# The two attention phases: the engines' programs written out straight instead of running in loops

## Chip, core and metric

The kernel runs on one core of one Trainium2 chip. Time is the device time of one launch, in microseconds (us); what stands for a version is the median of its runs. An engine's instructions run in the order in which its program gives them, and engines meet at semaphores.

## What is computed

The input is eight sequences of 512 tokens with 128 features. Two layers follow each other. Each adds to x an attention with 16 heads of 8 features, and a second branch. Layer 0 has an amplitude and phase attention, and beside it an attention over the batch followed by a mixture of eight experts; layer 1 has plain causal attention and a mixture of the best two of eight experts.

```
x = L0_attn_x
xn = _layernorm(x, axis=-1)
x = x + _L0_attn_ref(xn, ...) + _L0_ffn_ref(xn, ...)
xn = _layernorm(x, axis=-1)
x = x + _L1_attn_ref(xn, ...) + _L1_ffn_ref(xn, ...)
...
scores = jnp.where(mask[None, None], scores, -jnp.inf)     # causal, 512 x 512
attn = jax.nn.softmax(scores, axis=-1)
out = jnp.einsum('bhqk,bhkd->bhqd', attn, v)
```

## The kernel before

Seven phases run one after the other (`setup, mix0, middle0, attend0, middle1, experts1, attend1`), each a block that all engines enter and leave together. The change touches `attend0` and `attend1`, which are one function, `attend`, called with layer 0 or 1.

A **unit** is a group of four heads of one sequence. There are 32 (`UNITS`), four to a sequence, and a sequence is called a **row**. Every engine's program is cut into **steps**; step t does work for several units at once, at different depths of a pipeline:

- PE computes the scores of unit t that give each query's largest score (`maxima`, L2131 and the mask L2143), the scores of unit t-2 the other way round (`probabilities`, L2163), the product with the values for t-3 (`mix`, L2176), and turns the result of t-4 (`turn_mix`, L2184). At the end of a row it turns (L2190) and projects (`project`, L2196) the row's result.
- ACT takes ten exponentials of 128x512 in a step (L2089, unit t-2), and then copies the mixed result of t-3 (`mixT`, L2114). This copy stands once in each step, at its end, so its starts mark the steps. At the end of a row ACT also copies `contextT` (L2102). In layer 0 it makes, one row late, four normalised tiles (`z_norm`, L2107).
- DVE reduces the maxima (L2255, L2258, L2260, L2261), splits those of unit t-1 (`split_maxima`, L2271 and L2273) at the start of the step, copies them (L2280), divides (`divide`, L2287 and L2291), and ends a row with `add_row` (L2304; in layer 1 L2308), which adds the projection to x. In layer 0 it takes the statistics of the second norm as well.
- GpSimd (POOL) masks the exponentials (L2052), copies the values (L2060), and issues one indirect DMA in a step of layer 0 (L2068), two in layer 1. In layer 0, once in a row, it follows this with an addition over 128x512 (`second_norm`, L2022).
- SyncE (SP) loads the stacked q and k of unit t (L1973) and moves the maxima of t-3 into place (L1963).

GpSimd's program has always been written out, step by step. The other four use `in_steps`: the first steps straight, then a loop on the engine whose body is 8 steps (two rows), then the rest straight. For PE, ACT and DVE steps 0 to 7 are straight, 8 to 31 are three passes of the loop, and what follows is straight. SP does so too in layer 1; in layer 0 its steps 0 to 15 are straight and 16 to 31 are two passes. Step numbers of this text are those of t. In a loop the pass's number is in a register, so that a wait for a count that grows with the unit needs its target computed first, and so does an address that depends on the row:

```
    with eng.Fori(0, turns) as i:
        for phase in range(cycle):
            step(Unit(i + first // cycle, phase, cycle))
...
        dve.wait_ge(x_in[u.row_par].sem, (r - u.row_par) * 8 + 16)
        dve.tensor_tensor(k.x_sum[:, here, :], proj, x_tile[:, u.row_par, :, :], ALU.add).then_inc(added.sem, 1)
```

Of the kernel before, what the change touches and what calls it, by code (L numbers as in the profile page):

```python
# [43 lines left out]
NG = NH // GH  # L44
# [103 lines left out]
def in_steps(eng, units, depth, step, cycle=2, first=4):  # L148

    turns = (units - first) // cycle
    for t in range(first):
        step(Unit(t // cycle, t % cycle, cycle))
    with eng.Fori(0, turns) as i:
        for phase in range(cycle):
            step(Unit(i + first // cycle, phase, cycle))
    for t in range(first + cycle * turns, units + depth - 1):
        step(Unit(t // cycle, t % cycle, cycle))


def active(t, k, units):

    return not isinstance(t.turn, int) or 0 <= t.n - k < units
# [1698 lines left out]
def attend(nc, k, layer):  # L1863
# [5 lines left out]
    UNITS = B * NG  # L1869
# [7 lines left out]
    with ExitStack() as ctx:  # L1877
# [40 lines left out]
        DEPTH = 6  # L1918
        Z_AFTER = 12
# [35 lines left out]
        def _(sp):  # L1955
# [35 lines left out]
                    sp.dma_start(k.out[bass.ds(u.row, 1), :, :].rearrange("b (j p) d -> p (b j) d", p=P),  # L1991
                                 k.x_sum[:, bass.ds(u.row * QT, QT), :]).then_inc(stored[u.row_par].sem, 16)

            if layer == 0:
                in_steps(sp, UNITS, Z_AFTER + 1, step, 2 * NG, 4 * NG)
            else:
                in_steps(sp, UNITS, DEPTH + 1, step, 2 * NG, 2 * NG)
            if layer == 1:
                for i in range(2):
                    sp.wait_ge(stored[i].sem, B // 2 * 16)  # L2000
# [82 lines left out]
        @block.scalar  # L2083
        def _(act):
            def exponentials(u, c, side):
                act.wait_ge(prob_ps.sem, prob_ps.after(u, 2 * c + side))
                if c == 0 and side == 0 and u.past(2):
                    act.wait_ge(mixed.sem, mixed.done(u - 2))
                act.activation(probs[:, u.par, 2 * c + side, :], ps[:, PROB + side, :], ACT.Exp, scale=SCALE ** -2)\  # L2089
                   .then_inc(exped.sem, 1)  # L2090

            def step(t):
                row_ends = active(t, 4, UNITS) and (t - 4).group == NG - 1
                for c in range(SCH):
                    if active(t, 2, UNITS):
                        for side in range(2):
                            exponentials(t - 2, c, side)
                    if c == 3 and row_ends:
                        r = (t - 4).row
                        act.wait_ge(context_turned.sem, context_turned.done(r))  # L2100

                        act.copy(contextT[:, :], ps[:, TURN, :]).then_inc(contextT_ready.sem, 1)  # L2102
                    if c == 1 and layer == 0 and active(t, 6, UNITS) and (t - 6).group == NG - 1:
                        r = (t - 6).row
                        act.wait_ge(z_shift_done.sem, z_shift_done.done(r))
                        for j in range(QT):
                            act.activation(z_norm[:, j, :], z_sum[:, j, :], ACT.Identity, bias=z_shift[:, j:j + 1],  # L2107
                                           scale=z_rstd[:, j:j + 1]).then_inc(z_normed.sem, 1)
                if active(t, 3, UNITS):
                    u = t - 3  # L2110
                    act.wait_ge(mixed.sem, mixed.done(u))
                    if u.past(1):
                        act.wait_ge(mix_turned.sem, mix_turned.done(u - 1))
                    act.copy(mixT[:, :], ps[:, MIX, :]).then_inc(mixT_ready.sem, 1)  # L2114

            in_steps(act, UNITS, DEPTH + 1 - layer, step, 2 * NG, 2 * NG)

        @block.tensor
        def _(pe):
# [119 lines left out]
                    if c == 4 and row_ends:  # L2239
                        project(t - 4)  # L2240

            in_steps(pe, UNITS, DEPTH, step, 2 * NG, 2 * NG)

        @block.vector
        def _(dve):
# [64 lines left out]
            def step(t):  # L2310
                z_row = layer == 0 and active(t, 5, UNITS) and (t - 5).group == NG - 1
                if active(t, 1, UNITS):
                    split_maxima(t - 1)
                for c in range(MCH):
                    if active(t, 0, UNITS):
                        reduce(t, c)
                    if c == 0 and active(t, 4, UNITS):
                        divide(t - 4)
                    if c == 1 and active(t, 1, UNITS):
                        copy_maxima(t - 1)  # L2320
                    if c == 2 and z_row:
                        ln_stats(dve, z_sum, z_stats, z_mv, z_stats_done, z_mv_done, (t - 5).row, z_summed)
                    if c == 4 and z_row:
                        r = (t - 5).row
                        dve.wait_ge(z_rstd_done.sem, z_rstd_done.done(r))
                        dve.scalar_tensor_tensor(out=z_shift[:, :], in0=z_mv[:, :, 0], scalar=-1.0, in1=z_rstd[:, :],
                                                 op0=ALU.mult, op1=ALU.mult).then_inc(z_shift_done.sem, 1)
                if active(t, 4, UNITS) and (t - 4).group == NG - 1:
                    add_row(t - 4)

            in_steps(dve, UNITS, DEPTH, step, 2 * NG, 2 * NG)


def attend0(nc, k):
# [81 lines left out]
```

## Time and profile before

| | us |
|---|---|
| median of 3 runs (1272.55 to 1272.88) | 1272.88 |
| the profiled execution's own time | 1268.47 |
| its span, first to last instruction | 1266.9 |
| PE busy (77% of the span) | 981.7 |
| DVE busy (65%) | 819.4 |
| ACT busy (55%) | 690.9 |
| POOL busy (46%) | 582.5 |

The span is what the trace covers; 1.6 us of the profiled execution lie outside it. An engine counts as busy in its instructions proper, and not in those that compute registers, wait or branch, so these show only as time in which the engine stands still. The two attentions run from about 388 to 673 us and from about 1000 to the end. The granted TensorE clock averages 0.897 of full speed over the span.

### The profile page before, as it was taken

The numbers are of one execution on the slowest core, as the hardware profiler recorded it, in microseconds if no ns is written. First come the engines' busy times: TensorE is split into PE (matmuls) and PEld (weight loads), VectorE is DVE, ScalarE is ACT, GpSimd is POOL, SyncE is SP. The second block draws the span as 40 slices with busy tenths as digits, with TensorE's granted clock in tenths as the row PEclk, the third lists the DMA queues.
The fourth block names the chain that finished last, engine by engine and source line by source line (L and its number), as shares of the span: only waits on it lengthen the run. The fifth ranks groups of instructions, "written<-read, shape, count | busy, mean of one in ns | idle before, by whom it ended". The sixth has DMA issues, their size and how long they took to land. (4 is left out here: it accounts for less than half of the span.)

```text
span 1266.9 us, 27743 instructions
## 1 busy us (share of the span) xinstructions
PE 981.7 (77%) x8908; PEld 647.1 (51%) x8908; DVE 819.4 (65%) x1770; ACT 690.9 (55%) x1325; POOL 582.5 (46%) x793
## 2 busy tenths in 40 slices
PE   3789652989867988888872655199999599999987
PEld 1456431777753544444431433188888345555553
DVE  1566341667748999999943776133333699999992
ACT  1366343878714777677763454022222277777775
POOL 3467537010112565565551466411110367777775
PEclk9899776999985999999996666599999599999999
DMA  4321042577752222222201434456665112211111
GB/s 134 108 51 51 26 118 74 160 210 225 208 172 77 80 69 69 72 76 62 73 24 36 115 115 119 142 164 194 185 192 163 39 46 54 55 52 51 51 45 30
DMA packets 151735, 126.30 MB, mean 100 GB/s; under 512 B 23760, under 2 KB 134272, under 8 KB 151648
## 3 DMA queue, kind: packets, MB, share of 16 engines
q1 hardware_dynamic: 141904, 107.05, 29.5%
q0 software_dynamic: 8016, 17.71, 4.8%
q8 instruction: 44, 0.72, 0.2%
q10 hardware_dynamic: 1728, 0.46, 0.2%
q14 instruction: 43, 0.35, 0.1%
HBM read 77.83 MB, written 44.70 MB: 97 GB/s over the span
## 5 line engine op out<-in xcount | busy, mean ns | idle before, releaser
L2089 ACT ACTIVATE attend_probs<-attend_attend_ps 128x512 f32<-128x512 f32 x640 | 351.1, 600 | 161.7 <-PE attend_attend_ps L2163 154.4
L2163 PE MATMUL attend_attend_ps<-attend_q,attend_ks 50*128 50x512 f16 (+3 forms) x1024 | 236.5, 307 | 20.1 <-ACT attend_probs L2089 18.0
L2052 POOL TENSOR_SCALAR_AFFINE_SELECT attend_probs<-attend_probs 128x512 f32<-128x512 f32 x256 | 158.7, 637 | 159.5 <-ACT attend_probs L2089 158.6
L2131 PE MATMUL attend_attend_ps<-attend_ks,attend_q 48*128 48x512 f16 (+3 forms) x1024 | 191.3, 317 | 25.5 <-DMA attend_ks<-k_stack 16.2
L2176 PE MATMUL attend_attend_ps<-attend_probs,attend_vals 128*32 128x512 f32 (+3 forms) x2048 | 178.9, 446 | 0.0
L2258 DVE TENSOR_REDUCE attend_neg_max<-attend_attend_ps 128x2 f32<-128x1024 f32 x128 | 155.0, 1211 | 9.9 <-PE attend_attend_ps L2143 9.8
L2143 PE MATMUL attend_attend_ps<-identb,stairs 64*128 64x128 bf16 (+1 forms) x1280 | 144.3, 213 | 0.0
L2163 PEld LDWEIGHTS attend_attend_ps<-attend_q,attend_ks 50*128 50x128 f16 x1024 | 70.9, 94 | 116.1 <-ACT attend_probs L2089 93.2
L2260 DVE TENSOR_REDUCE attend_neg_max<-attend_attend_ps 128x2 f32<-128x768 f32 x128 | 121.8, 951 | 9.2 <-PE attend_attend_ps L2143 8.4
L1800 DVE TENSOR_TENSOR experts_hidden<-experts_experts_ps,experts_gate 128x512 f32<-128x512 f32 x39 | 27.0, 691 | 136.3 <-ACT experts_gate L1779 136.3
L2143 PEld LDWEIGHTS attend_attend_ps<-identb,stairs 64*128 64x128 bf16 x1280 | 105.9, 100 | 17.5 <-issue 4.7
L1834 PE MATMUL experts_experts_ps<-experts_rowsT,experts_w_in 128*128 128x256 f32 (+1 forms) x468 | 110.1, 385 | 1.6 <-ACT experts_rowsT L1787 1.5
L1104 POOL DMA_INDIRECT sorted<-middle_scaled,rank_row x64 | 66.6, 1040 | 58.1 <-issue 28.9
L1834 PEld LDWEIGHTS experts_experts_ps<-experts_rowsT,experts_w_in 128*128 128x128 f32 (+1 forms) x468 | 82.4, 183 | 17.6 <-ACT experts_rowsT L1787 2.1
L1779 ACT ACTIVATE experts_gate<-experts_experts_ps 128x512 f32<-128x512 f32 x39 | 23.3, 597 | 120.8 <-PE experts_experts_ps L1834 120.8
L1766 POOL DMA_DIRECT2D experts_rows<-sorted x39 | 27.7, 712 | 131.8 <-issue 131.8
L2131 PEld LDWEIGHTS attend_attend_ps<-attend_ks,attend_q 48*128 48x128 f16 x1024 | 67.2, 96 | 39.0 <-DMA attend_ks<-k_stack 16.6
L2255 DVE TENSOR_REDUCE attend_neg_max<-attend_attend_ps 128x4 f32<-128x1024 f32 x64 | 78.3, 1224 | 8.5 <-PE attend_attend_ps L2143 8.5
L1430 POOL TENSOR_TENSOR x_sum<-middle_amp_n,middle_sine 128x1024 f32<-128x1024 f32 x8 | 18.9, 2365 | 118.4 <-DVE middle_amp_n L1636 118.3
L2068 POOL DMA_INDIRECT attend_moe<-done,back_row x64 | 61.6, 962 | 14.9 <-issue 14.9
L1846 PE MATMUL experts_experts_ps<-experts_w_out,experts_hidden 128*128 128x128 f32 (+1 forms) x468 | 58.7, 275 | 0.9 <-DVE experts_result L1811 0.9
L2176 PEld LDWEIGHTS attend_attend_ps<-attend_probs,attend_vals 128*32 128x32 f32 x2048 | 44.7, 109 | 22.8 <-issue 5.9
(319 smaller groups left out, 1950.7 us busy)
## 6 DMA issues: line engine op xcount, KB each, us to landing
experts_w_in<-in_L_ffn_w_dram SPq DMA_DIRECT2D x78, 176.0 KB, 2.4
q_stack<-middle_parts SPq DMA_DIRECT2D x24, 256.0 KB, 3.3
k_stack<-middle_parts SPq DMA_DIRECT2D x24, 256.0 KB, 3.6
attend_q<-q_stack SPq DMA_DIRECT2D x64, 96.0 KB, 2.2
attend_ks<-k_stack SPq DMA_DIRECT2D x64, 96.0 KB, 2.2
middle_w_in<-in_L_ffn_W_dram SPq DMA_DIRECT2D x23, 256.0 KB, 2.7
middle_w_out<-in_L_ffn_W_dram SPq DMA_DIRECT2D x23, 256.0 KB, 3.1
experts_rows<-sorted POOLq DMA_DIRECT2D x39, 128.0 KB, 2.5
```

The source lines that it names most:

```text
L1104: pool.indirect_dma_start(k.sorted1, bass.IndirectOffsetOnAxis(ap=k.rank_row[:, c * NT + tile:c * NT + tile + 1], axis=0), scaled[:, c, ti ...
L1834: mm = pe.matmul(ps[0:size[c], hidden_bank(u, bank), half * ROWS:(half + 1) * ROWS], w_in[:, u.phase, w + c * P:w + c * P + size[c]], rows ...
L2052: pool.affine_select(out=block_, in_=block_, compare_op=ALU.is_ge, fill=0.0, base=0, pattern=[[0, GH], [1, P]], channel_multiplier=-1).the ...
L2068: pool.indirect_dma_start(moe[:, c * NT + n, :], None, src, bass.IndirectOffsetOnAxis(ap=at_row[:, c * NT + n:c * NT + n + 1], axis=0))\
L2089: act.activation(probs[:, u.par, 2 * c + side, :], ps[:, PROB + side, :], ACT.Exp, scale=SCALE ** -2)\
L2131: pe.matmul(ps[:, bank + side, col:col + (qt + 1) * P], q[rows(side, KR), g, pair, qt * P:(qt + 1) * P], ks[rows(side, KR), g, pair, 0:(qt ...
L2143: mm = pe.matmul(span[:, :, col:col + 64], k.stairs[here, stair:stair + P], k.identb[here, here].unsqueeze(1).broadcast_to([64, len(blocks ...
L2163: mm = pe.matmul(ps[:, PROB + side, col:col + S - kt * P], ks[rows(side, KM), g, pair, kt * P:(kt + 1) * P], q[rows(side, KM), g, pair, kt ...
L2176: mm = pe.matmul(ps[32 * h:32 * h + 32, MIX, kt * P:S], vals[:, u.par, kt * GH + h, :], probs[:, u.par, 2 * c + h % 2, col:col + S - kt * ...
L2255: ins = dve.tensor_reduce(out[:, :, :, 1], pair_banks.rearrange("p s (h t) -> p s h t", h=HP), X_AXIS, ALU.max, negate=True)
L2258: ins = dve.tensor_reduce(out[:, :, c // 2, 3], pair_banks, X_AXIS, ALU.max, negate=True)
L2260: dve.tensor_reduce(out[:, :, c // 2, 2], pair_banks[:, :, 0:384], X_AXIS, ALU.max, negate=True)
```

## The change

The loop is dropped from the four programs that used it: each step is given constant numbers. The loops of other phases stay.

```diff
@@ -156,6 +156,11 @@
     for t in range(first + cycle * turns, units + depth - 1):
         step(Unit(t // cycle, t % cycle, cycle))
 
 
+def all_steps(units, depth, step, cycle):
+    for t in range(units + depth - 1):
+        step(Unit(t // cycle, t % cycle, cycle))
+
+
...
-            if layer == 0:
-                in_steps(sp, UNITS, Z_AFTER + 1, step, 2 * NG, 4 * NG)
-            else:
-                in_steps(sp, UNITS, DEPTH + 1, step, 2 * NG, 2 * NG)
+            all_steps(UNITS, Z_AFTER + 1 if layer == 0 else DEPTH + 1, step, 2 * NG)
...
-            in_steps(act, UNITS, DEPTH + 1 - layer, step, 2 * NG, 2 * NG)
+            all_steps(UNITS, DEPTH + 1 - layer, step, 2 * NG)
...
-            in_steps(pe, UNITS, DEPTH, step, 2 * NG, 2 * NG)
+            all_steps(UNITS, DEPTH, step, 2 * NG)
...
-            in_steps(dve, UNITS, DEPTH, step, 2 * NG, 2 * NG)
+            all_steps(UNITS, DEPTH, step, 2 * NG)
```

No instruction that computes changes its place. What goes are the register instructions (REGISTER_ALU, and ISA, which is several of them in one) and the branches. In the lists that follow, a semaphore has the name under which its number was first used. On DVE, the end of the loop's last step, which ends a row, and the start of the next step before the change (here `setup_raw_in7` is `projected`, `setup_raw_in5` is `x_in`, and `setup_scale_ready` is `max_turned`):

```order
L2255 TENSOR_REDUCE attend0_neg_max<-attend0_attend_ps 128x4 [waits attend0_scored]
L2299 ISA
L2303 ISA [waits setup_raw_in7]
L2304 ISA [waits setup_raw_in5]
L2304 TENSOR_TENSOR x_sum<-attend0_attend_ps,attend0_x_tile 128x512
L155 REGISTER_ALU
L155 COMPARE_AND_BRANCH
```

At the loop's top stand two more before the first instruction of `split_maxima`:

```order
L155 ISA
L2270 ISA [waits setup_scale_ready]
L2271 TENSOR_SCALAR attend0_max_parts<-attend0_neg_max 128x2x8 [waits setup_roots_ready]
```

The same place on DVE in the changed kernel, where lines after 1990 stand 2 further down:

```order
L2257 TENSOR_REDUCE attend0_neg_max<-attend0_attend_ps 128x4 [waits attend0_scored]
L2306 TENSOR_TENSOR x_sum<-attend0_attend_ps,attend0_x_tile 128x512 [waits setup_raw_in5,setup_raw_in7]
L2273 TENSOR_SCALAR attend0_max_parts<-attend0_neg_max 128x2x8 [waits setup_roots_ready,setup_scale_ready]
L2275 SCALAR_TENSOR_TENSOR attend0_max_parts<-attend0_neg_max,attend0_max_parts 128x2x8 [waits setup_norms_ready]
```

The three register instructions between the reduction and the addition are gone, and the waits stand on the addition itself. On PE, the loop's top with the start of its first step before the change (`setup_turned` is `max_in`, `setup_raw_in6` is `added`, `setup_copied` is `context_done`):

```order
L155 ISA
L2160 ISA [waits setup_turned]
L2163 MATMUL attend0_attend_ps<-attend0_q,attend0_ks 128x512 [waits setup_cols_in]
L2124 ISA
L2126 ISA [waits attend0_loaded0]
L2131 MATMUL attend0_attend_ps<-attend0_ks,attend0_q 128x512 [waits setup_roots_ready]
L2131 MATMUL attend0_attend_ps<-attend0_ks,attend0_q 128x512
L2143 MATMUL attend0_attend_ps<-identb,stairs 128x64 x4
L2163 MATMUL attend0_attend_ps<-attend0_q,attend0_ks 128x512 [waits setup_cols_in]
L2204 REGISTER_ALU
L2208 ISA [waits setup_copied]
L2182 REGISTER_ALU [waits setup_raw_in6]
```

The same stretch of PE in the changed kernel, with the instruction that comes next:

```order
L2165 MATMUL attend0_attend_ps<-attend0_q,attend0_ks 128x512 [waits setup_cols_in,setup_turned]
L2133 MATMUL attend0_attend_ps<-attend0_ks,attend0_q 128x512 [waits setup_roots_ready,attend0_loaded0]
L2133 MATMUL attend0_attend_ps<-attend0_ks,attend0_q 128x512
L2145 MATMUL attend0_attend_ps<-identb,stairs 128x64 x4
L2165 MATMUL attend0_attend_ps<-attend0_q,attend0_ks 128x512 [waits setup_cols_in]
L2186 MATMUL attend0_attend_ps<-ident,attend0_mixT 128x128 [waits setup_raw_in13,setup_raw_in6,setup_copied]
```

Seven register instructions are gone, and every wait stands on the matmul it is for.

## Rows read from the trace of the kernel before

**Rows 1.** Waits by engine (us in total, times, longest us): ACT's largest.

```profile
ACT attend_probs L2089 <- PE attend_attend_ps L2163: 154.4, 203, 24.6
```

**Rows 2.** Waits of SP's queue, the largest.

```profile
SPq L1963 <- DVE attend_maxT L2280: 197.7, 64, 7.7
```

**Rows 3.** Timeline of ACT, layer 0: start us, us, instruction. Steps 5 to 24.

```profile
425.12 0.59 ACT L2114 COPY attend_mixT<-attend_attend_ps 128x512 f32<-128x512 f32 x1
432.36 0.59 ACT L2114 COPY attend_mixT<-attend_attend_ps 128x512 f32<-128x512 f32 x1
...
440.17 0.61 ACT L2114 COPY attend_mixT<-attend_attend_ps 128x512 f32<-128x512 f32 x1
...
448.04 0.59 ACT L2114 COPY attend_mixT<-attend_attend_ps 128x512 f32<-128x512 f32 x1
...
456.46 0.59 ACT L2114 COPY attend_mixT<-attend_attend_ps 128x512 f32<-128x512 f32 x1
...
472.56 0.61 ACT L2114 COPY attend_mixT<-attend_attend_ps 128x512 f32<-128x512 f32 x1
...
480.51 0.59 ACT L2114 COPY attend_mixT<-attend_attend_ps 128x512 f32<-128x512 f32 x1
...
489.56 0.59 ACT L2114 COPY attend_mixT<-attend_attend_ps 128x512 f32<-128x512 f32 x1
...
505.57 0.61 ACT L2114 COPY attend_mixT<-attend_attend_ps 128x512 f32<-128x512 f32 x1
...
515.64 0.59 ACT L2114 COPY attend_mixT<-attend_attend_ps 128x512 f32<-128x512 f32 x1
...
573.74 0.61 ACT L2114 COPY attend_mixT<-attend_attend_ps 128x512 f32<-128x512 f32 x1
...
583.50 0.59 ACT L2114 COPY attend_mixT<-attend_attend_ps 128x512 f32<-128x512 f32 x1
```

**Rows 4.** Timeline of ACT, layer 1, steps 11 to 13.

```profile
1083.97 0.61 ACT L2114 COPY attend_mixT<-attend_attend_ps 128x512 f32<-128x512 f32 x1
...
1091.96 0.59 ACT L2114 COPY attend_mixT<-attend_attend_ps 128x512 f32<-128x512 f32 x1
...
1099.21 0.59 ACT L2114 COPY attend_mixT<-attend_attend_ps 128x512 f32<-128x512 f32 x1
```

**Rows 5.** Timelines of ACT and DVE, ends of rows at steps 7 and 11.

```profile
438.72 0.59 ACT L2102 COPY attend_contextT<-attend_attend_ps 128x512 f32<-128x512 f32 x1
...
440.71 0.68 DVE L2304 TENSOR_TENSOR x_sum<-attend_attend_ps,attend_x_tile 128x512 f32<-128x512 f32 x1
...
471.10 0.59 ACT L2102 COPY attend_contextT<-attend_attend_ps 128x512 f32<-128x512 f32 x1
...
473.23 0.69 DVE L2304 TENSOR_TENSOR x_sum<-attend_attend_ps,attend_x_tile 128x512 f32 x1
```

**Rows 6.** Timelines of DVE and POOL, starts of steps 12, 16, 24 and 32.

```profile
473.79 0.97 POOL L2068 DMA_INDIRECT attend_moe<-done,rank_row  x1 [0.16 <-issue]
474.04 0.17 DVE L2273 SCALAR_TENSOR_TENSOR attend_max_parts<-attend_neg_max,attend_max_parts 128x16 f16<-128x16 f32 x1
...
506.81 0.97 POOL L2068 DMA_INDIRECT attend_moe<-done,rank_row  x1 [0.16 <-issue]
507.27 1.86 DVE L2271 TENSOR_SCALAR attend_max_parts<-attend_neg_max 128x16 f16<-128x16 f32 x1
...
575.35 1.93 DVE L2273 SCALAR_TENSOR_TENSOR attend_max_parts<-attend_neg_max,attend_max_parts 128x16 f16<-128x16 f32 x1
...
643.23 1.96 DVE L2273 SCALAR_TENSOR_TENSOR attend_max_parts<-attend_neg_max,attend_max_parts 128x16 f16<-128x16 f32 x1
```

**Rows 7.** PE's loop branch (count, ns least, median, most), all loops of the program.

```profile
L155 PEldq COMPARE_BRANCH  x13: 76/208/234, 504.9 to 1239.6; - x13
```

**Rows 8.** DMA queues, 410 to 510 us, then 511 to 641: packets, MB, share.

```profile
q8 instruction: 9, 0.15, 0.6%
...
q14 instruction: 2, 0.02, 0.0%
```

## The prediction, made before the changed kernel ran

> **What bounds the kernel now.** I read the waits first. ACT's largest wait is for PE's second scores, 154.4 us in 203 pieces [rows 1]: in the attentions PE and ACT run as a ring, in which an exponential waits for its scores and the next scores wait for the exponential to free their bank. DVE stands in that ring once in a step, since PE waits for its quotients, split maxima and, at a row's end, its addition. SP's queue waits 197.7 us for DVE, at most 7.7 us at a time [rows 2]; it is early everywhere.
>
> Then I measured the ring, from one `mixT` copy of ACT to the next, which is one step. A plain step takes 432.36 - 425.12 = 7.24 us in the straight part of layer 0 [rows 3], and 1099.21 - 1091.96 = 7.25 us inside the loop of layer 1 [rows 4]. PE, ACT and DVE compute registers before nearly every wait in the second and never in the first. So in a plain step all of them lie under other work: an engine's queue computes them while its last instruction runs. What a loop costs has to be looked for where an engine comes late to a wait that is already met, which is at the ends of rows.
>
> **The end of a row.** PE projects, DVE adds (L2304), and PE waits for that addition in the next step before `turn_mix`. From the start of ACT's `contextT` copy to the start of the addition it takes 440.71 - 438.72 = 1.99 us at step 7, which is straight, and 473.23 - 471.10 = 2.13 us at step 11, in the loop [rows 5]: 0.14 us for the register instructions that stand between the projection and the addition. The step that follows takes 448.04 - 440.17 = 7.87 us at step 8 and 480.51 - 472.56 = 7.95 us at step 12 [rows 3], in layer 1 at step 12 1091.96 - 1083.97 = 7.99 us [rows 4]. Step 8 still pays the way into the loop, so it is an upper bound of the straight step; 7.95 - 0.14 = 7.81 less what the loop adds on PE's side is the other bound. I take 7.80, a saving of 0.15 to 0.19 us, say 0.18, at each of steps 12, 16, 20, 24, 28 and 32 of both layers: **12 x 0.18 = 2.2 us**.
>
> **The turn of the loop.** PE's branch takes 208 ns in the median and 76 at the least, which is one not taken [rows 7]; PE turns twice in each attention, and a row's end is where it happens. I allow 0.08 us for each of the 4 turns and 0.08 for each of the 2 ways in: **0.5 us**. But in layer 0 the turning steps take far more: step 16 is 515.64 - 505.57 = 10.07 us and step 24 is 583.50 - 573.74 = 9.76, against 7.95 for step 12, which is the same step in the middle of the body [rows 3]. This is not the branch. At step 12 POOL starts its indirect DMA at 473.79, and the second instruction of DVE's split starts 0.25 us later and takes 0.17 us. At step 16 DVE's first one comes 0.46 us after the DMA's start and takes 1.86 us for the same 16 columns; at step 24 the DMA, by the same 1.23 us behind `mixT` as at step 12, starts at 574.97, and DVE's second one comes 0.38 us behind and takes 1.93; at step 32 the same instruction takes 1.96 [rows 3, 6]. POOL goes from the DMA straight into its 128x512 addition, and the DVE instruction ends when that ends. So there is a cliff somewhere between 0.25 and 0.38 us behind the DMA's start: DVE ahead of it runs at once, and DVE behind it waits for both of POOL's instructions, with PE and ACT waiting behind DVE. POOL's program has no loop and keeps its distance from ACT. DVE's register instructions push it over.
>
> Without them DVE is 0.14 us earlier than at step 12, which puts its second instruction at 0.25 - 0.14 = 0.11 us, well ahead of the cliff, in all rows. Steps 16 and 24 then cost what step 12 does: 10.07 - 7.95 = 2.12 and 9.76 - 7.95 = 1.81 us. At step 32 the pipeline drains and PE has no maxima to compute, so part of the stall is slack; between nothing and 1.8 us I take half, 0.9. **Together 4.8 us**, no part of which is counted above, where these steps give only their 0.18.
>
> The Trainium skill (SBUF — State Buffer, Who interferes with whom) says that DVE and GpSimd share a pair of SBUF ports under an exclusive lock that whoever starts first holds for its whole instruction. The two waits of nearly 2 us agree with a lock. That the lock is held from the DMA's start does not agree with step 12, where DVE ran in 0.17 us inside it; by that rule DVE would be stopped at 0.11 us as well, nothing of the 4.8 us would come back, and the sum would be 2.7. The measured step decides.
>
> **SP, ACT and the rest.** SP loses its address computations beside each DMA; its 197.7 us of waiting cover them [rows 2]. ACT's register instructions lie under exponentials of 0.6 us, by the plain steps above: nothing. If that cover were gone, plain steps would differ between loop and straight, and they do not. The fill of the pipeline (steps 0 to 7) and its drain are straight already.
>
> **What is added is code to fetch.** An instruction queue, q8, moved 9 packets from 410 to 510 us, while code ran for the first time, and none from 511 to 641, in the second and third pass, where only q14 appears with 2 [rows 8]. So the body was there already, and the straight program must bring in about 9 more packets per 100 us of it: some 13 in each attention, 26 in all. Their share of 0.6% of 16 engines over 100 us is 1.07 us for each packet. They come about 11 us apart, and the plain step of 7.24 us lies in the stretch with fetches. So I cost them at nothing; what hides them is that a packet is wanted only 10 us after the last.
>
> **Sum.** 2.2 + 0.5 + 4.8 = 7.5 us, less 0.3 for small new stalls where engines meet earlier than before: 7.2. From the profiled execution's 1268.47 this gives 1261.3. The median of the runs is 4.4 us above that execution, which the trace does not explain; taken off the median, **1265.7 us**.
>
> **A race that can go either way.** Step 9 takes 456.46 - 448.04 = 8.42 us, step 13 489.56 - 480.51 = 9.05 [rows 3]. They hold the same work, and DVE and POOL want to go at the same moment there; five of the six such steps are long. The change moves neither against the other, since both hang on DVE's statistics. All six may come out short (3.2 us less) or all long (0.6 more).
>
> **Rivals.**
> - *The collision stays.* Another delay, or the cliff lying lower, keeps DVE behind POOL in the same three steps: 2.2 + 0.5 = 2.7 us, 1270.2. For it speaks that only an interval of 0.13 us is known to hold the cliff; against it, that steps 8 and 12 both pass. Chance 0.09.
> - *More collisions go than the trace shows.* Steps 12, 20 and 28 stand at most 0.13 us ahead of the cliff, and the unprofiled runs are 4.4 us longer, which is about two more collisions of 2.1. Then 4.2 more come back: 1261.5. Chance 0.12.
> - *Slower: the fetch stalls PE.* Should each of the 26 new packets keep PE waiting for its 1.07 us, that is 28 us against 7.2 of gain: 1293. It decides from 7.2 / 26 = 0.28 us per packet. Against it speaks the plain step with fetches. Chance 0.06.
> - *The loop's turn costs a fetch.* The Trainium skill (Runtime: NRT & Kernel Launch, Instruction fetch mechanics) says that a taken branch to code outside a small window waits for a DMA fetch. For four turns of PE at 1.07 us this kernel would lose 4.3 us that the change returns, beside the 7.2: 1261.4. No q8 packet in the passes and a branch of at most 234 ns speak against it [rows 7, 8]. Chance 0.02.
> - *Nothing to be seen:* the stalls move elsewhere in the ring, and the time stays within 2.5 us. Chance 0.06.
>
> That leaves 0.65 for the forecast, with a range of its own of 1262 to 1268. Over all, 1259 to 1271 holds eight in ten: below it lie more collisions together with a won race, above it the fetch. A measurement of this kernel tells about 0.2%, 2.5 us, from no change. Faster by more is the forecast, the two cases that give more, and half of the first rival: 0.84. Within it 0.10, slower 0.06.
>
> **What would show it.** In the profile after, steps 16 and 24 of layer 0 last 7.8 us, and L2273 and L2275 (the split's new lines) stay under 0.3 us at the starts of rows; the addition begins 1.99 us behind `contextT` at every row's end; plain steps stay at 7.24; q8 has about 70 packets instead of 44. I am wrong if plain steps grow, if a 1.9 us instruction of the split turns up at a row's start, or if PE stands idle around q8's packets for a reason that no semaphore gives.

## The result, and the profile after

The changed kernel takes 1263.9 us in the median of 6 runs (1263.0 to 1266.6), the kernel before beside it on the same chip (A) 1272.6 (6 runs, 1270.6 to 1272.9). The ratio is 0.9939 [0.9927, 0.9952], which is 7.8 us less.

The profiled execution took 1266.19 us with a span of 1264.6, only 2.3 us less than the one profiled before. The page of the changed kernel, the lines that moved:

```profile
span 1264.6 us, 25739 instructions
...
PE 987.7 (78%) x8908; PEld 649.9 (51%) x8908; DVE 810.1 (64%) x1770; ACT 691.2 (55%) x1325; POOL 580.4 (46%) x793
...
q8 instruction: 67, 1.10, 0.4%
```

The profile before counts 27743 instructions, so some 2000 register instructions and branches are gone, and the instructions proper have kept their numbers. DVE is 9.3 us less busy with the same 1770 instructions. Of that, 7.0 us are in the two instructions of the split (30.7 + 15.9 us before, 25.9 + 13.7 after), which are as many as before and were held less. q8 moved 23 packets more.

Timeline of ACT in the changed kernel (start us, us, instruction), layer 0: `contextT` and `mixT` of step 7, `mixT` of steps 8, 9, 11, 12, 13, then `contextT` and `mixT` of step 15, `mixT` of 16, 23 and 24:

```profile
440.24 0.59 ACT L2104 COPY attend_contextT<-attend_attend_ps 128x512 f32<-128x512 f32 x1
...
441.69 0.61 ACT L2116 COPY attend_mixT<-attend_attend_ps 128x512 f32<-128x512 f32 x1
...
449.50 0.59 ACT L2116 COPY attend_mixT<-attend_attend_ps 128x512 f32<-128x512 f32 x1
...
457.89 0.59 ACT L2116 COPY attend_mixT<-attend_attend_ps 128x512 f32<-128x512 f32 x1
...
473.87 0.61 ACT L2116 COPY attend_mixT<-attend_attend_ps 128x512 f32<-128x512 f32 x1
...
481.68 0.59 ACT L2116 COPY attend_mixT<-attend_attend_ps 128x512 f32<-128x512 f32 x1
...
490.67 0.59 ACT L2116 COPY attend_mixT<-attend_attend_ps 128x512 f32<-128x512 f32 x1
...
505.20 0.59 ACT L2104 COPY attend_contextT<-attend_attend_ps 128x512 f32<-128x512 f32 x1
...
506.65 0.61 ACT L2116 COPY attend_mixT<-attend_attend_ps 128x512 f32<-128x512 f32 x1
...
514.46 0.59 ACT L2116 COPY attend_mixT<-attend_attend_ps 128x512 f32<-128x512 f32 x1
...
572.18 0.61 ACT L2116 COPY attend_mixT<-attend_attend_ps 128x512 f32<-128x512 f32 x1
...
580.00 0.59 ACT L2116 COPY attend_mixT<-attend_attend_ps 128x512 f32<-128x512 f32 x1
```

From one `mixT` start to the next: step 8 takes 449.50 - 441.69 = 7.81 us, step 12 also 7.81, step 16 514.46 - 506.65 = 7.81 where it took 10.07, step 24 7.82 where it took 9.76 [rows 3]. All ends of rows now look like step 8. Step 13 takes 490.67 - 481.68 = 8.99 against 9.05 [rows 3].

Timelines of DVE and POOL in the changed kernel, start of step 16, in order of time:

```profile
507.19 0.68 DVE L2306 TENSOR_TENSOR x_sum<-attend_attend_ps,attend_x_tile 128x512 f32<-128x512 f32 x1
507.79 0.17 DVE L2273 TENSOR_SCALAR attend_max_parts<-attend_neg_max 128x16 f16<-128x16 f32 x1
507.88 0.97 POOL L2070 DMA_INDIRECT attend_moe<-done,rank_row  x1 [0.16 <-issue]
507.99 0.17 DVE L2275 SCALAR_TENSOR_TENSOR attend_max_parts<-attend_neg_max,attend_max_parts 128x16 f16<-128x16 f32 x1
508.88 1.29 POOL L2024 TENSOR_TENSOR attend_z_sum<-y_all,attend_moe 128x512 f32<-128x512 f32 x1
```

The addition starts 507.19 - 505.20 = 1.99 us behind `contextT`, and the second instruction of the split 0.11 us behind the DMA's start. The two instructions of the split last 0.17 us each, where L2271 lasted 1.86 [rows 6]. The second comes 0.10 to 0.11 us behind the DMA's start in all seven rows.

Where the time went, from the same `mixT` starts and the ends of the spans, in us. "After" is the execution above, the last two columns are profiled executions of both kernels on two slower chips that the experiments used:

| stretch | before | after | before, chip B | after, chip D |
|---|---|---|---|---|
| start to step 3 of layer 0 | 410.7 | 412.2 | 411.9 | 412.1 |
| layer 0, steps 8 to 32 | 209.8 | 203.4 | 209.9 | 204.0 |
| layer 0, steps 33 and 34 | 11.6 | 13.3 | 11.6 | 14.2 |
| to step 3 of layer 1 | 360.8 | 361.9 | 364.1 | 362.9 |
| layer 1, steps 8 to 32 | 195.0 | 193.5 | 210.2 | 204.1 |
| layer 1, steps 33 and 34 | 10.7 | 12.0 | 13.5 | 12.1 |

On the first chip the steps give 6.4 + 1.4 = 7.8 us. In this execution 2.9 of them are given back in the drains, where the pipeline empties, and 2.6 in stretches whose code did not change; the first stretch alone differs by up to 9 us between executions with the same code in it (406.1 to 415.2 over the runs below), which is why a difference of two single executions says little here.

The drain of layer 0, the stretch from the second last `mixT` copy to the last, as granted clock (`PEclk`, 1.00 is 2.4 GHz) and busy time of each engine. Before:

```profile
core 0: us, PE busy (x) PEld busy (x) DVE busy (x) ACT busy (x) POOL busy (x), PEclk, DMA share, GB/s
657.80:661.60 3.80, 2.92 (x36) 1.31 (x36) 0.55 (x2) 0.67 (x3) 3.51 (x4) 1.00 0.00 0
```

After:

```profile
652.91:658.33 5.42, 4.61 (x36) 1.84 (x36) 0.55 (x2) 0.60 (x3) 4.37 (x4) 0.69 0.07 17
```

The same 36 matmuls take 4.61 us of PE instead of 2.92, and the granted clock averages 0.69 over the stretch, which is 1.2 GHz for more than half of it, instead of 2.4 GHz throughout (1.00). In the second drain it is 0.79 from 1244.2 to 1252.5.

### The profile page after: what moved, and what is told of

It reads as the page before. It is cut to its first block and busy times, and to the rows that moved or that the text cites. A ratio compares the mean times of both kernels' runs of the same rounds, so it can differ in the third digit from the quotient of the medians.

```text
span 1264.6 us, 25739 instructions
## 1 busy us (share of the span) xinstructions
PE 987.7 (78%) x8908; PEld 649.9 (51%) x8908; DVE 810.1 (64%) x1770; ACT 691.2 (55%) x1325; POOL 580.4 (46%) x793
## 5 line engine op out<-in xcount | busy, mean ns | idle before, releaser
L2260 DVE TENSOR_REDUCE attend_neg_max<-attend_attend_ps 128x2 f32<-128x1024 f32 x128 | 155.0, 1211 | 10.2 <-PE attend_attend_ps L2145 10.1
```

The lines of the kernel that those rows point to most:

```text
L2260: ins = dve.tensor_reduce(out[:, :, c // 2, 3], pair_banks, X_AXIS, ALU.max, negate=True)
```

## The experiments

Eleven runs followed on three chips more: eight edited kernels, the kernel before once and the changed kernel twice. Each ratio is against the kernel before on the same chip, which took 1291.4 us on that of the first four (chip B), 1270.2 on that of the next four (C) and 1292.5 on that of the last three (D).

**e1, DVE alone straight.** On the kernel before, one of the four programs changed:

```diff
-            in_steps(dve, UNITS, DEPTH, step, 2 * NG, 2 * NG)
+            all_steps(UNITS, DEPTH, step, 2 * NG)
```

> The kernel before with DVE's two attention programs alone written out straight; PE, ACT and SP keep their loops. My theory (DVE's register instructions at a row's end make it miss the gap before GpSimd's addition): the addition starts 1.99 us behind contextT at every row's end, steps 16 and 24 of layer 0 fall from 10.07 and 9.76 us to about 7.9, no instruction of the split over 1 us at a row's start, and most of the gain is here: 5.5 to 7 us, 1265.5 to 1267 against a before of 1272.6. Rival (the loop's turn itself, above all PE's branch, costs the time): steps 16 and 24 stay near 10 us and the time within 2 us of before.

Measured: 1285.3, ratio 0.9941 [0.9919, 0.9963]. ACT's timeline, `mixT` of steps 15 and 16 of layer 0, then of 14 and 15 of layer 1:

```profile
506.25 0.61 ACT L2119 COPY attend_mixT<-attend_attend_ps 128x512 f32<-128x512 f32 x1
...
514.12 0.59 ACT L2119 COPY attend_mixT<-attend_attend_ps 128x512 f32<-128x512 f32 x1
...
1112.07 0.59 ACT L2119 COPY attend_mixT<-attend_attend_ps 128x512 f32<-128x512 f32 x1
...
1122.36 0.62 ACT L2119 COPY attend_mixT<-attend_attend_ps 128x512 f32<-128x512 f32 x1
```

Step 16 takes 7.87 us with PE, ACT and SP still looping. DVE's loop alone was what put it into the collisions. The 0.06 us above 7.81 is what remains of the turn on the other engines. Layer 1's step 15, which ends a row, takes 10.29 us here. On the first chip it took 8.78 before the change:

```profile
1106.44 0.59 ACT L2114 COPY attend_mixT<-attend_attend_ps 128x512 f32<-128x512 f32 x1
...
1115.22 0.61 ACT L2114 COPY attend_mixT<-attend_attend_ps 128x512 f32<-128x512 f32 x1
```

So layer 1 runs in another regime on this chip, of which the runs below show more.

**e2, all straight but DVE.** On the changed kernel, DVE's call turned back.

```diff
-            all_steps(UNITS, DEPTH, step, 2 * NG)
+            in_steps(dve, UNITS, DEPTH, step, 2 * NG, 2 * NG)
```

> The changed kernel with DVE's programs alone put back into the loop; PE, ACT and SP are straight. My theory: DVE is late again, x is added 2.13 us behind contextT in the loop and 2.25 at its turn, steps 16, 24 and 32 of layer 0 collide and steps 16 and 24 last 9.7 us or more; the time is within 2 us of before, 1270.5 to 1272.5. Rival (what PE, ACT and SP no longer compute gives the gain): steps 16 and 24 near 7.9 us, about 1266.

Measured: 1287.3, ratio 0.9956 [0.9932, 0.9981]. ACT's timeline at the same four places, with DVE's split instruction at the start of step 16:

```profile
505.03 0.61 ACT L2116 COPY attend_mixT<-attend_attend_ps 128x512 f32<-128x512 f32 x1
...
506.73 1.85 DVE L2273 TENSOR_SCALAR attend_max_parts<-attend_neg_max 128x16 f16<-128x16 f32 x1
...
514.93 0.59 ACT L2116 COPY attend_mixT<-attend_attend_ps 128x512 f32<-128x512 f32 x1
...
1113.58 0.59 ACT L2116 COPY attend_mixT<-attend_attend_ps 128x512 f32<-128x512 f32 x1
...
1123.08 0.62 ACT L2116 COPY attend_mixT<-attend_attend_ps 128x512 f32<-128x512 f32 x1
```

In layer 0 it is the kernel before: step 16 takes 9.90 us, with 1.85 in the split, step 24 takes 9.64, and steps 8 to 32 take 209.3 together. With e1 this settles the 4.8 us of layer 0. The time did not stay near that of before, as I had expected, for a reason in layer 1: its step 15 takes 9.50 us instead of the 10.29 of e1, and of the other five steps of the loop that end a row four take the same; one, step 19, takes 10.18.

**e3, a sweep over the cliff.** In the changed kernel DVE writes a single column of a spare tile r times behind the addition of row r, to come later by a little more each row.

```diff
+                    for n in range(r):
+                        dve.memset(pad[:, 4 * n:4 * n + 1], 0.0)
```

> The changed kernel with r tiny writes of one column (memset) put on DVE behind the addition that ends row r of layer 0, r from 0 to 7, so that DVE starts the split later and later from row to row; everything else as it was. If each takes about 60 ns, the split's second instruction comes 0.10, 0.16, 0.22, 0.28, 0.34, 0.40 and 0.46 us behind the start of GpSimd's indirect DMA. Theory (a cliff between 0.25 and 0.38 us): steps 8, 12, 16 stay at 7.8 to 7.9 us, and from some row on between the fourth and the fifth a split instruction takes 1.9 us and the step 9.7 or more, all later rows too. Rival (the time lost grows with DVE's lateness, no cliff): each row-end step is 0.06 us longer than the one before and none jumps.

Measured in one profiled execution: 1286.3. Each write took only some 10 ns, so the second split instruction came 0.10 to 0.16 us behind the DMA's start, none was held, and all those steps stayed at 7.81 to 7.82. It says nothing of the cliff; e6 repeats it with five times the writes.

**before_again.** The kernel before, unchanged.

> The kernel before, unchanged, for a second profile: the unprofiled median of before lies 4.1 us above its profiled execution. If the collisions of layer 0 differ from execution to execution, more row-end steps than 16, 24 and 32 last 9.7 us or more here. If the clock makes the difference, the steps are the same and the granted clock or the phases outside the attentions differ. If neither differs, profiling itself makes the executions shorter. Time: 1270.5 to 1273, ratio 1.00.

Measured: 1292.6, ratio 0.9995 [0.997, 1.002]. ACT's timeline, layer 1, `mixT` of steps 13 to 15:

```profile
1109.35 0.59 ACT L2114 COPY attend_mixT<-attend_attend_ps 128x512 f32<-128x512 f32 x1
...
1117.15 0.59 ACT L2114 COPY attend_mixT<-attend_attend_ps 128x512 f32<-128x512 f32 x1
...
1127.41 0.62 ACT L2114 COPY attend_mixT<-attend_attend_ps 128x512 f32<-128x512 f32 x1
```

In layer 0 the same three steps collide as in the first profile, by the same amounts (10.04, 9.78, 8.35 us), and no others. So the collisions are a fixed pattern. Layer 1 is slower here: step 14, a plain one, takes 7.80 us, and step 15, which ends a row, 10.26, where the first chip had 7.23 and 8.78. The steps behind the ends of rows are no longer than on the first chip (7.95 to 8.01 us against 7.98 to 8.06). Step 7 ends a row too, but in the part that is straight in this kernel as well, and takes 9.51. The granted clock is 1.00 in this stretch on both chips, so it is not that.

**after_again.** The changed kernel, unchanged.

> The changed kernel once more, beside runs of before on the same chip. On the chip of the first four experiments layer 1 ran differently from the first profiles: a plain step took 7.75 us and not 7.23, and the step that ends a row 10.27 us with PE and ACT in loops against 9.50 without. If this is a property of the chip, then on such a chip the change gains the two parts together, near 1.0%, and on one like the first 0.6%. If it comes from profiling or from one kernel's code, layer 1 is as in the first profile after, wherever this runs. The drain steps (33 and 34) were 3 us longer in the first profile after, with the clock at 1.2 GHz there; if that is the change's doing it shows again here.

Measured: 1262.8, ratio 0.9947 [0.9928, 0.9965]. Every step from 8 to 32 of both layers is within 0.02 us of the first profile of the changed kernel, and the last step of layer 0 takes 5.32 us again instead of 3.72: the lower clock in the drains comes back with it.

**e4, the second norm's work moved later.** The race of steps 9, 13, 17 and so on was to be taken apart: in the changed kernel POOL computes the reciprocal deviation behind its masks, ACT makes `z_norm` at its fourth place in the step, not its second, and DVE computes the shift one step later.

```diff
                 pool.tensor_tensor(z_sum[:, :, :], k.y[:, here, :], moe[:, here, :], ALU.add).then_inc(z_summed.sem, 1)
-                ln_rstd(pool, k, z_mv, z_ve, z_rstd, z_mv_done, z_eps_done, z_rstd_done, r)
...
+                if layer == 0 and n >= 6 and (n - 6) % NG == 0:
+                    ln_rstd(pool, k, z_mv, z_ve, z_rstd, z_mv_done, z_eps_done, z_rstd_done, (n - 6) // NG)
...
-                    if c == 1 and layer == 0 and active(t, 6, UNITS) and (t - 6).group == NG - 1:
+                    if c == 3 and layer == 0 and active(t, 6, UNITS) and (t - 6).group == NG - 1:
```

> The changed kernel with the second norm of layer 0 moved off the start of the step after a row's end: GpSimd computes z_rstd after the masks of its unit instead of before them, DVE makes z_shift in the next step behind its second reduction and no longer ahead of the split, ACT normalises two chunks later. Theory (in steps 13, 17, 21, 25 and 29 the split waits for GpSimd's masks, which stand one behind the other there because z_rstd held them up): these steps fall from 8.98 us to 8.4 or less and the split's first instruction takes under 0.3 us; 3 us less than the changed kernel, 0.25%. Rival (the long step is ACT's four extra tiles and no wait for DVE): no change, or slower because the norm is used later.

Measured: 1265.7, ratio 0.9976 [0.9959, 0.9992], 2.9 us above the changed kernel on the same chip. DVE's timeline, start of step 13:

```profile
479.53 0.17 DVE L2274 TENSOR_SCALAR attend_max_parts<-attend_neg_max 128x16 f16<-128x16 f32 x1
479.74 0.17 DVE L2276 SCALAR_TENSOR_TENSOR attend_max_parts<-attend_neg_max,attend_max_parts 128x16 f16<-128x16 f32 x1
```

In the changed kernel these two take 0.68 and 0.55 us here; now no instruction of the split is held anywhere in layer 0. Yet step 13 still takes 9.0 us. Step 9 became as long, steps 10, 14, 22 and 26 grew from 8.16 to 8.8, and 18 and 30 fell to 7.2. The theory had these steps at 8.4 us or less once the split runs free, and they are not; the edit moved work of ACT too, so it does not price the hold by itself. The rival, ACT's four extra tiles (1.64 us of ACT in such a step), is left and fits, but no run leaves them out.

**e5, the addition away from the DMA.** On the kernel before, with all its loops, POOL's `second_norm` goes behind the step's first mask.

```diff
-                if layer == 0 and n >= 6 and (n - 6) % NG == 0:
-                    second_norm((n - 6) // NG)
-                if n < UNITS:
-                    for i in range(QT):
+                for i in range(QT):
+                    if n < UNITS:
                         mask(n, i)
+                    if i == 0 and layer == 0 and n >= 6 and (n - 6) % NG == 0:
+                        second_norm((n - 6) // NG)
```

> The kernel before, all loops kept, with one thing changed on GpSimd: in layer 0 its 128x512 addition and what follows of the norm stand behind the first mask of the step and no longer directly behind the indirect DMA. Theory (DVE, late, waits for the DMA and for the addition that follows without a gap): the split still comes late at steps 16, 24 and 32 but waits for the rest of the DMA at most, 0.6 us instead of 1.9, or not at all if only the addition holds it up; steps 16 and 24 last 8.0 to 8.6 us instead of 10.0 and 9.8, 3 to 5 us less in all, 0.3%. Rival (the loop's turn costs it by itself): they stay near 10 us.

Measured: 1265.2, ratio 0.9967 [0.995, 0.9983]. Timelines of DVE, POOL and ACT around the start of step 16, with `mixT` of steps 15 and 16 first and last:

```profile
507.01 0.61 ACT L2114 COPY attend_mixT<-attend_attend_ps 128x512 f32<-128x512 f32 x1
...
508.24 0.97 POOL L2068 DMA_INDIRECT attend_moe<-done,rank_row  x1 [0.16 <-issue]
...
508.70 0.17 DVE L2271 TENSOR_SCALAR attend_max_parts<-attend_neg_max 128x16 f16<-128x16 f32 x1
508.91 0.18 DVE L2273 SCALAR_TENSOR_TENSOR attend_max_parts<-attend_neg_max,attend_max_parts 128x16 f16<-128x16 f32 x1
...
511.63 1.28 POOL L2022 TENSOR_TENSOR attend_z_sum<-y_all,attend_moe 128x512 f32<-128x512 f32 x1
...
515.40 0.59 ACT L2114 COPY attend_mixT<-attend_attend_ps 128x512 f32<-128x512 f32 x1
```

DVE comes 0.46 us behind the DMA's start, exactly as late as in the collision of before [rows 6], and runs in 0.17 us; the second comes 0.67 behind and runs in 0.18. The DMA does not hold DVE at all. What held it was the addition queued behind the DMA; whether another GpSimd instruction in that place would hold it too was not tried. Step 16 takes 8.39 us instead of 10.07, which is 0.43 more than step 12; DVE still comes late there. Steps 8 to 32 of layer 0 take 203.9, nearly what the change itself reaches, while the loops still run; part of that is in steps 13, 17 and so on. Step 13 fell from 9.05 to 8.70.

**e6, the sweep again.** As e3 with `range(5 * r)`.

> As e3_sweep, where one tiny write delayed DVE by only some 10 ns, so that no row reached the cliff; here 5r of them behind the end of row r: the split's second instruction about 0.10, 0.15, 0.20, 0.25, 0.30, 0.35 and 0.40 us behind the DMA's start. Theory: none of the first four is held, the last one is, and every row behind the first held one too; the held step lasts 9.7 us or more against 7.8. Rival (no cliff): the steps grow by 0.05 us each.

Measured in one profiled execution: 1271.3. Timelines of POOL and DVE at the start of step 16 and of step 20:

```profile
506.68 0.97 POOL L2071 DMA_INDIRECT attend_moe<-done,rank_row  x1 [0.16 <-issue]
...
506.93 0.18 DVE L2276 SCALAR_TENSOR_TENSOR attend_max_parts<-attend_neg_max,attend_max_parts 128x16 f16<-128x16 f32 x1
...
539.61 0.97 POOL L2071 DMA_INDIRECT attend_moe<-done,rank_row  x1 [0.16 <-issue]
...
539.94 1.99 DVE L2276 SCALAR_TENSOR_TENSOR attend_max_parts<-attend_neg_max,attend_max_parts 128x16 f16<-128x16 f32 x1
...
540.60 1.29 POOL L2025 TENSOR_TENSOR attend_z_sum<-y_all,attend_moe 128x512 f32<-128x512 f32 x1
```

At 0.25 us behind the DMA's start it runs in 0.18 us and the step takes 7.82; at 0.33 us it is held 1.99 us, until the addition has ended (539.94 + 1.99 = 541.93 against 540.60 + 1.29 = 541.89), and the step takes 9.64. The next two rows come at 0.42 and 0.46 us and take 9.64 each, and in the last the first split instruction already comes at 0.33 us and is held. Less than 0.1 us of delay costs 1.8 us. But this sweep has only the step from 10 writes to 15 there, and e8 below finds that 15 writes delay DVE by themselves. Free of such writes, the trace of the kernel before has the bounds 0.26 us (not held, step 28) and 0.37 (held, step 32).

The Trainium skill (SBUF — State Buffer, Who interferes with whom) has an exclusive lock between DVE and GpSimd, which whoever issues first holds for the whole instruction. The trace agrees that one waits until the other's instruction has ended. Taken by the starts in the trace, the rule does not hold: at 539.94 DVE was there 0.66 us before the addition started, with nothing but the DMA running on POOL. Whether the addition counted as issued by then, behind the DMA, no run shows.

**e7, both.** The changed kernel with the edit of e5.

> The changed kernel with the move of e5 on top: GpSimd's 128x512 addition of layer 0 stands behind the first mask. Theory: steps 16, 24 and 32 have no collision to lose any more, so only the steps after a row's end gain: in e5 step 13 took 8.70 us against 9.05 before, so steps 13, 17, 21, 25 and 29 fall from 8.98 to about 8.7, 1.5 us in all; about 0.7% under the kernel before, 1261 where that takes 1270. Rival: the race of these steps falls the other way and nothing is gained, the same as the changed kernel.

Measured: 1274.1, ratio 0.9857 [0.9834, 0.988], the best of all. ACT's timeline, steps 12 and 13 of layer 0:

```profile
476.66 0.59 ACT L2116 COPY attend_mixT<-attend_attend_ps 128x512 f32<-128x512 f32 x1
...
485.30 0.59 ACT L2116 COPY attend_mixT<-attend_attend_ps 128x512 f32<-128x512 f32 x1
```

Step 13 takes 8.64 us where the changed kernel has 8.98, and steps 8 to 32 of layer 0 take 201.7, 2.3 less than in the changed kernel on this chip. That is all that the profile puts down to the edit. The medians are 7.0 us apart; the rest isn't traced to it (this execution's stretch ahead of layer 0's step 3 was 407.1 against 412.1, and that code is the same). Two of the steps that end a row in layer 1, 15 and 23, took 10.2 us here and not 9.5.

**after_third.** The changed kernel on the same chip as e7.

> The changed kernel, unchanged, beside e7 on the same chip: ratio 0.994 to the kernel before; in the profile the steps of the first one, 7.81 us behind each row's end.

Measured: 1281.1, ratio 0.9915 [0.9887, 0.9943], 11.0 us less than before by the ratio, more than on the first chip. The table above has where: against the kernel before on chip B, which is as slow, 5.9 us come from layer 0 and 6.1 from layer 1 instead of 1.4. Layer 1's steps 11, 15 and so on take 9.51 us instead of 10.27. In layer 0 the steps behind the ends of rows are those of the first profile, as expected, but step 9 is long this time, 8.97 us.

**e8, the sweep with the addition moved.** The edits of e6 and e5 together, on the changed kernel.

> The delays of e6 with the move of e5: GpSimd issues its indirect DMA in the same place, but a mask follows and not the addition. If the addition holds DVE up before it has started, none of the seven rows is held, at any delay, and the steps behind the ends of rows grow smoothly from 7.8 to about 8.1 us. If the DMA itself has a part in it (its writing of descriptors), the rows from 0.34 us on are still held, for 0.6 us at most.

Measured in one profiled execution: 1277.2. Timelines of POOL and DVE at the start of step 24:

```profile
567.23 0.97 POOL L2071 DMA_INDIRECT attend_moe<-done,rank_row  x1 [0.16 <-issue]
567.44 0.17 DVE L2274 TENSOR_SCALAR attend_max_parts<-attend_neg_max 128x16 f16<-128x16 f32 x1
...
568.57 0.17 DVE L2276 SCALAR_TENSOR_TENSOR attend_max_parts<-attend_neg_max,attend_max_parts 128x16 f16<-128x16 f32 x1 [0.95 <-DVE attend_max_parts L2274]
...
570.06 1.27 POOL L2025 TENSOR_TENSOR attend_z_sum<-y_all,attend_moe 128x512 f32<-128x512 f32 x1
```

No instruction of the split was held for 1.9 us, in any row, which agrees with e5. But from the fourth row on, whose writes are 15 and more, DVE is late without a holder: here the second instruction starts 0.95 us behind the end of the first, and starts while POOL stands idle between the DMA's end at 568.20 and its next mask at 569.46. Steps 20 to 32 take 8.07, 8.83, 8.99 and 7.52. I put that down to the burst of tiny writes, which no run shows by itself, so the later rows of this sweep tell nothing of the lock. The smooth growth to 8.1 us that I had expected did not come. In e6 the delay had another form, one long instruction that ends with POOL's addition, in every row from the fourth on.

## Why the prediction was right, step by step

**The collisions (4.8 us) were right in size.** Steps 16, 24 and 32 gave 10.07 - 7.81 = 2.26, 9.76 - 7.82 = 1.94 and 8.34 - 7.35 = 0.99 us, 5.2 together with the row-end saving in them, against 2.12 + 1.81 + 0.9 and 0.18 each, 5.4. The two experiments on DVE alone show the cause: its loop made it late for the cliff, and the loops of the others had no part in it.

What in DVE's loop is less clear than I wrote. "DVE's register instructions push it over" does not say why they push at steps 16, 24 and 32 only. At the ends of rows in the middle of the loop's body the addition comes 2.13 us behind `contextT` [rows 5], 0.14 late, and DVE passes. At the ends of passes it comes 2.50, 2.25 and 2.24 us behind, before the turn itself. Timelines of ACT and DVE before the change, end of step 15:

```profile
504.12 0.59 ACT L2102 COPY attend_contextT<-attend_attend_ps 128x512 f32<-128x512 f32 x1
...
506.62 0.69 DVE L2304 TENSOR_TENSOR x_sum<-attend_attend_ps,attend_x_tile 128x512 f32 x1 [0.42 <-issue]
```

The extra 0.37 and 0.11 us decide the collisions. The profile names nothing that DVE waited for there, and what takes them stays open.

**The mechanism of the cliff was half right.** "DVE behind it waits for both of POOL's instructions" is the step that failed. e5 and e6 show that DVE waits for the addition only, that the DMA holds nothing, and that the addition holds DVE from some 0.3 us behind the DMA's start, some 0.6 us before the addition itself starts. The cliff lies between 0.26 and 0.37 us, inside my 0.25 to 0.38; e6 has it below 0.33, if its writes have no part in that. It made no difference to the sum, since DVE came to 0.11, but it does to the remedy.

**The end of a row (12 x 0.18 = 2.2 us)** gave 7.96 - 7.81 = 0.15 in layer 0's steps 12, 20 and 28, and 0.12 to 0.25 in layer 1; with 0.03 in each row-end step there, layer 1 gave 1.4 us in all. `x_sum` came 1.99 us behind `contextT` at every row, as said.

**The turn of the loop (0.5 us):** e1 leaves PE's turn in and pays 0.06 us at step 16. For PE, ACT and SP the allowance of 0.08 was near; DVE's own lateness at the turns is in the collisions above.

**Nothing for fetching was right.** q8 moved 23 packets more, not 26, and the plain step stayed at 7.23 us. From 511 to 637 us, where the loop had fetched nothing, the changed kernel shows

```profile
q8 instruction: 12, 0.20, 0.6%
q14 instruction: 6, 0.05, 0.2%
```

and every step there is as short as it was, or shorter. The rival that made each packet cost PE 1.07 us is refuted. So is that of the turn that costs a fetch: e1 keeps PE's loop, and its turning steps 16 and 24 take 7.87 us where straight ones take 7.81. By the Trainium skill (Runtime: NRT & Kernel Launch, Instruction fetch mechanics) a taken branch waits for a DMA fetch when its target lies outside a window of two pages of 256 instructions each; the same section gives PE room for 2048 instructions. A step has at least 84 matmuls (1024 + 1024 + 2048 + 1280 for 64 units), so PE's body of 8 steps is longer than the window. The trace agrees with the 2048 and not with the window: no packet of q8 in the passes [rows 8], and 0.06 us for a turn.

**"Less 0.3 for small new stalls"** was too small in the profiled executions: 2.9 us, all of it in the drains, where the granted clock fell to 1.2 GHz. In layer 0's drain it stayed at 2.4 GHz in the kernel before, in both its profiles, and in e2, which are the three with steps 16, 24 and 32 and no others held; it fell in the ten others, in step 33, in 34 or in both. e5 is among these, with its loops kept, so it does not go with the loops. Nor does it go with the held steps alone, since e6, which had steps 20, 24, 28 and 32 held, fell too. In layer 1 it is mixed: it fell in the second profile of before and not in the first. Why it falls is open.

**Why 1263.9 and not 1265.7.** The steps gave 7.8 us against 7.2 predicted, and the medians differ by 7.8 to 8.7. If every execution gave back the drains' 2.9 us, the medians should differ by 5 only. The kernel before ran 4.1 us above its profiled execution, the changed one 2.3 us below its own. Of the changed kernel's six executions the profiled one has the lowest mean granted clock, 0.888 against 0.892 to 0.896, and is the second longest. On chip B the 24 executions of the kernel before spread from 1286.9 to 1296.5 us, with 0.899 in the shortest and 0.890 and 0.891 in the two longest. So single executions can't say more; what makes up the 3 us stays open. That "more collisions go than the trace shows" is not the answer: before_again shows the same three in another execution.

**The race** went as before in the first two profiles of the changed kernel, with step 9 short (8.39) and the other five at 8.96 to 8.99. In the third all six were long, which is the 0.6 us named as the worse end. In e4 the split is not held and they are as long; moving the addition (e5, e7) takes 0.35 us off each of the five.

**What I had not seen: layer 1 has two regimes.** On chips B and D its plain step takes 7.7 to 7.8 us and the step that ends a row 10.27, and there the change takes 0.76 off each of the latter. The prediction had put nothing on these steps. It is owed to PE, ACT or SP written out straight, since e2 has it and e1 does not; which of the three was not tried apart, and it is not certain in each row, since one such step of e2 and two of e7 took 10.2. What makes these chips slower in this layer is open. So the gain depends on the chip: by the ratios 7.8 us on A, 6.7 on C and 11.0 on D.

**What is left.** The three collisions were not the only holds. In layer 0 of the changed kernel 17 instructions of the split still take 0.48 to 1.14 us instead of 0.17, and in layer 1 L2275 takes 1.15 us seven times, once for a row, up to the end of a GpSimd addition over 128x512 that had started just before it. e4, which had none left in layer 0, shows that removing them need not shorten the steps.

## What to carry to other kernels

Look for the cost of a loop where an engine comes late to a wait already met, and not where it has cover: here some 2000 register instructions and branches cost nothing in plain steps, 0.15 us at the end of a row, and 2 us where DVE, another 0.1 us or more late at the end of a pass, came with a 16-column instruction behind a 128x512 GpSimd addition. A short instruction that now and then lasts 2 us, and ends with one on another engine, is the sign of it; it can be cured on either side, and moving the long instruction away (e5) leaves more room than being 0.2 us early. A difference of two single profiled executions can miss most of a gain of 0.6%: sum the stretches that the change touches, and judge the whole by medians.

## What the runs showed of the hardware

- GpSimd's addition holds DVE before it starts, while it is still queued behind its own engine's indirect DMA (held at 0.37 us behind the DMA's start and later, and in e6 at 0.33; not at 0.26 or before). The DMA itself does not hold DVE's two split instructions (0.17 and 0.18 us in e5, 0.46 and 0.67 us behind its start).
- The granted clock can fall to 1.2 GHz in the few microseconds of a pipeline's drain and stretch the same 36 matmuls from 2.92 to 4.61 us of PE.
- Single-column DVE writes (128x1) cost some 10 ns each in e3, but DVE stalled behind bursts of 15 and more of them (0.95 us in the row shown), for a reason not found.
- The same kernel took 1270 to 1273 us on two chips (A and C) and 1291 to 1293 on two others, most of it in one layer (210.2 on chip B against 195.0 us on A in steps 8 to 32 of layer 1), at a granted clock of 1.00.
